# Second cross attention of a two-layer decoder: products in three float32r parts, transposes in row halves, outputs one step later

## Chip, cores and metric

The kernel runs on 1 core of one Trainium2 chip. The metric is the device time in microseconds (us), median of several runs. The whole program, two decoder layers, is one launch; the change is in one of its six stages.

## The reference

x is 2 x 1024 x 256 in float32, ctx is 2 x 154 x 256. Each of six blocks is added to x: a gated delta-rule attention (A), a cross attention (B), experts (C); then a local attention (D), a second cross attention (E) and a mixture of 32 experts (F). The change is in E:

```
def _L1_xattn_ref(Q, K, V, attn_mask, Wq, bq, Wk, bk, Wv, bv, Wo, bo):   # H = 256, NH = 16 heads, DK = 16
    q, k, v = proj(Q, Wq, bq), proj(K, Wk, bk), proj(V, Wv, bv)           # to (b, NH, S, DK)
    scores = jnp.einsum('bhqd,bhkd->bhqk', q, k) / jnp.sqrt(jnp.float32(DK))
    scores = jnp.where(attn_mask[:, None, :, :], jnp.float32(-1000000000.0), scores)
    attn = jax.nn.softmax(scores, axis=-1)
    ctx = jnp.einsum('bhqk,bhkd->bhqd', attn, v)
    return ctx.transpose(0, 2, 1, 3).reshape(b, -1, NH * DK) @ Wo.T + bo
x = x + _L1_xattn_ref(_layernorm(x, axis=-1), ctx_1024, ctx_1024, mask, ...)
```

## The kernel before

The stages run in the order A to F. Every engine walks through the same written list `order` and does its part of each entry, so the order of the list is the order of every engine's queue; engines wait for each other by semaphores. Stage E works on 16 tiles n of 128 rows of x, in 32 steps g: step g holds 8 of the 16 heads of tile g // 2, as two groups j of four heads, and r = 0 to 3 names the four heads of a group, which lie at partitions 32 r. Each head is padded to 32 rows, so the query weights are 256 x 512.

What the entries of `order` do:

- `key`, `value`: products of ctx with the weights, once. `query n4, m`: 128 of the 512 query columns for four tiles, 2 products of 512 columns in float32; ScalarE adds the bias and writes Q. Each float32 product shows in the trace as two matmuls.
- `score g`: for each r a mask product (L2417) into bank r and then the scores of 8 heads (L2425). VectorE takes the maxima of the four banks (L2491); `exp g, r` is ScalarE's exponential, two instructions for each r (L2542), into P. Bank r is free for the next step once its exp is done.
- `turn g, r`: 4 transposes of P (L2436) into one bank; ScalarE copies r = 0, 1 to PT, VectorE r = 2, 3 (L2497). `mix g`: 32 matmuls of values by PT (L2447), copied to OT by ScalarE; `across g`: two transposes back (L2455); VectorE divides by the sums (L2505, L2506) into AO.
- `flip n`: transposes of AO (L2461), copied to AOT by ScalarE (L2562). `out n`: the output product (L2466), added to X by VectorE (L2513).
- `stat`, `norm`, `ln` with the letter F: the layer norm for the next stage, two tiles at a time. `stat`: VectorE's statistics (L262, L265), then six small instructions of GpSimd (L284 to L221) that make rs. `norm`: VectorE's normalisation (L275), which waits for rs. `ln`: TensorE's transposes and ScalarE's copy to XT. The last pair of tiles of stage E's own layer norm is done inside E (`norm`, `ln` with the letter E).
- `bias`: GpSimd adds the output bias to X (L2577).

The scores use banks 0 to 3. Turns, mixes, flips, across, outputs, queries and layer norms use banks 4 to 7 in turn, each as one entry (`i = 4 + turns % 4`), and TensorE waits until the bank's last user has been emptied.

The steps are a software pipeline. In step g TensorE does turn g - 1 (r = 0, 1), mix g - 2, score g, in even steps flip n = g // 2 - 2, turn g - 1 (r = 2, 3), across g - 2, and then in even steps out n, in odd steps up to 23 a query. The four queries of the first tiles come right after the keys. Below, a step starts where its first mask product starts.

Stage B, the first cross attention, and stage F already have products in three float32r parts (L1283, L2676), and stage B has transposes in row halves (L1348), with 16 heads of 64.

## Time and profile before

| | us |
|---|---|
| median of 3 runs | 2528.76 (2523.03 to 2533.08) |
| the profiled execution | 2528.92 |
| its span | 2527.1 |
| stage E, first key product to last X add | 1694.94 to 1910.67 |
| TensorE busy over the whole span | 2246.4 (89%) |
| VectorE, ScalarE, GpSimd busy | 1596.7, 1165.5, 737.1 |
| mean granted clock of TensorE | 0.94 |

Times in the rows below are in us from the span's start. In a timeline row the columns are start, duration until the last of the instructions ends, engine, line, operation and tiles, count, and in brackets the engine's idle time before them and what ended it. PE is TensorE, PEld its weight loads, DVE VectorE, ACT ScalarE, POOL GpSimd.

### The profile page before, as it was taken

The page shows a single profiled execution, that of the slowest core. Times are in us where ns is not written, and L with a number is a line of the kernel's source. Part 1 is how long each engine was busy: PE and PEld are TensorE (multiplying, and loading weights), DVE is VectorE, ACT ScalarE, POOL GpSimd, SP SyncE. Part 2 cuts the span into 40 slices and gives each one's busy share as a digit, 9 for nine tenths or more (in the row PEclk, how much of TensorE's full clock was granted, in tenths as well). Part 3 has the DMA queues.
Part 4 walks back from the last instruction along what each step waited for, and adds up shares of the span by engine and source line. Part 5 has one row for each costly group of instructions (what it writes and reads, how often), then busy time and mean ns, then how long its engine had stood idle before and what let it go on. Part 6 is the DMA issues. An engine that isn't in the chain of part 4 may idle for free. (4 is left out here: it accounts for less than half of the span.)

```text
span 2527.1 us, 63640 instructions
## 1 busy us (share of the span) xinstructions
PE 2246.4 (89%) x26627; PEld 1868.0 (74%) x26627; DVE 1596.7 (63%) x3513; ACT 1165.5 (46%) x3240; POOL 737.1 (29%) x866
## 2 busy tenths in 40 slices
PE   5798989999898999946997689989997899999998
PEld 4677877777785888835886466667776788888887
DVE  6666676667653566546773455655666777777776
ACT  4435444443423777612553366656664233333332
POOL 2334243333423444331664523420101001110110
PEclk9799999999999999967999799999998899999999
DMA  5001010100101100021442300000000000000001
GB/s 162 1 11 36 27 36 11 36 27 11 66 3 60 62 19 19 19 76 39 123 108 47 88 2 2 2 2 2 2 2 20 13 26 26 26 21 24 26 7 34
DMA packets 87966, 83.44 MB, mean 33 GB/s; under 512 B 27264, under 2 KB 83456, under 8 KB 86272
## 3 DMA queue, kind: packets, MB, share of 16 engines
q1 hardware_dynamic: 81536, 70.98, 8.9%
q0 software_dynamic: 6144, 8.39, 2.0%
q8 instruction: 210, 3.44, 0.6%
q14 instruction: 76, 0.62, 0.1%
HBM read 68.71 MB, written 10.65 MB: 31 GB/s over the span
## 5 line engine op out<-in xcount | busy, mean ns | idle before, releaser
L2676 PE MATMUL bank<-f_XH,f_wp 128*128 128x512 f32 x1088 | 364.6, 396 | 5.9 <-DVE f_XL L2786 5.9
L797 DVE SCALAR_TENSOR_TENSOR a_acc<-a_praw,a_convw,a_acc 128x256 f32<-128x256 f32 x345 | 206.2, 599 | 99.2 <-ACT a_acc L957 91.0
L2676 PEld LDWEIGHTS bank<-f_XH,f_wp 128*128 128x128 f32 x1088 | 208.4, 192 | 48.5 <-issue 5.0
L2676 PEld LDWEIGHTS bank<-f_wp,f_Hp 128*128 128x128 f32 x1632 | 214.3, 191 | 27.5 <-DVE X L2813 16.0
L2676 PE MATMUL bank<-f_wp,f_Hp 128*128 128x256 f32 x1632 | 218.5, 283 | 16.2 <-DVE X L2813 15.4
L2676 PE MATMUL bank<-f_XL,f_wp 128*128 128x512 f32 x544 | 215.9, 397 | 0.0
L2860 POOL TENSOR_TENSOR f_wp<-wa,f_wp 128x768 fp32r<-128x768 f32 x34 | 62.9, 1850 | 521.5 <-ACT f_wp L2826 521.5
L2811 DVE SCALAR_TENSOR_TENSOR X<-bank,f_w,X 128x256 f32<-128x256 f32 x512 | 211.4, 476 | 0.0
L2849 ACT ACTIVATE f_Hp<-f_H 128x512 fp32r<-128x512 f32 x136 | 85.9, 632 | 223.8 <-DVE f_H L2798 223.8
L2847 ACT ACTIVATE f_G<-bank 128x512 f32<-128x512 f32 x136 | 81.3, 598 | 165.4 <-PE bank L2676 165.4
L594 PE MATMUL bank<-XT,wa 128*128 128x256 f32 x512 | 155.2, 434 | 0.3 <-ACT a_acc L957 0.3
L2800 DVE TENSOR_TENSOR f_Hp<-f_H,f_Hp 128x512 fp32r<-128x512 f32 x136 | 94.2, 692 | 94.9 <-ACT f_Hp L2849 94.9
L684 PE MATMUL bank<-wa 64*64 64x64 f32 x2560 | 108.1, 229 | 48.8 <-DVE wa L894 35.2
L2798 DVE TENSOR_TENSOR f_H<-bank,f_G 128x512 f32<-128x512 f32 x136 | 94.0, 691 | 80.0 <-PE bank L2676 80.0
L684 PEld LDWEIGHTS bank<-wa 64*64 64x64 f32 x2560 | 89.3, 139 | 72.6 <-DVE wa L894 45.5
L2156 DVE TENSOR_REDUCE d_mx<-bank 128x2 f32<-128x512 f32 (+1 forms) x128 | 75.2, 650 | 105.2 <-PE bank L2091 105.2
L1024 ACT ACTIVATE wa<-bank 128x256 f32<-128x256 f32 x160 | 58.4, 386 | 155.9 <-PE bank L684 155.1
L2226 ACT ACTIVATE d_P<-bank,d_mx 128x256 f32<-128x256 f32 (+1 forms) x256 | 95.0, 479 | 75.1 <-DVE d_mx L2156 75.1
L2676 PEld LDWEIGHTS bank<-f_XL,f_wp 128*128 128x128 f32 x544 | 104.7, 192 | 16.8
L894 DVE COPY_PREDICATED wa<-masks,bank 128x512 f32<-128x512 uint8 x128 | 91.4, 729 | 37.8 <-PE bank L698 37.5
L698 PE MATMUL bank<-wa 64*64 64x64 f32 x2560 | 112.2, 232 | 2.1 <-ACT wa L1024 2.1
L1509 POOL TENSOR_TENSOR b_P<-b_P,b_rec 128x616 f32<-128x616 f32 x64 | 77.7, 1213 | 116.6 <-DVE b_rec L1418 116.6
(390 smaller groups left out, 5520.2 us busy)
## 6 DMA issues: line engine op xcount, KB each, us to landing
wa<-in_c_w SPq DMA_DIRECT2D x64, 256.0 KB, 3.4
wa<-in_f_gu SPq DMA_DIRECT2D x34, 256.0 KB, 2.7
wb<-grown SPq DMA_DIRECT2D x4, 1536.0 KB, 7.0
a_KQg<-grown SPq DMA_DIRECT2D x4, 1536.0 KB, 6.5
wa<-in_f_d SPq DMA_DIRECT2D x34, 128.0 KB, 2.8
a_E<-decays SPq DMA_DIRECT2D x16, 256.0 KB, 4.0
X<-in_x SPq DMA_DIRECT2D x4, 512.0 KB, 5.2
wa<-in_a_wqkv SPq DMA_DIRECT2D x1, 2048.0 KB, 8.8
```

Source lines behind the costliest of these rows:

```text
L594: i = t.e.matmul(b.ap[:, 0:B * BT_].rearrange("p (b t) -> p b t", b=B), wqkv[:, j, c * P:(c + 1) * P], xt, start=j == 0, stop=j == KD - 1, ...
L684: i = t.e.matmul(heads(b.ap)[both(bb), h, :], nt[c % 2][both(bb), h, :], xx[c % 2][both(bb), 0, h, :], start=True, stop=True, tile_positio ...
L698: i = t.e.matmul(heads(b.ap[:, H * R:])[both(bb), h, :], y[both(bb), h, :], xt[both(bb), h, :], start=True, stop=True, tile_position=(bb * ...
L797: i = v.e.scalar_tensor_tensor(A_, praw[:, c, :, j:j + BT_], convw[:, c, j:j + 1], A_, ALU.mult, ALU.add)
L894: i = v.e.copy_predicated(xx[c % 2], masks[:, l].unsqueeze(2).broadcast_to([P, 2, H, R]), b.ap.rearrange("p (w h r) -> p w h r", w=2, h=H))
L2226: i = c.e.activation(Pm[of(g, r)][:, j, lo:], pair(b.ap)[:, j, lo:], ACT.Exp, bias=mx[:, of(g, r), j:j + 1])
L2676: i = t.e.matmul(out_, lhsT[x], rhs[y], start=n == 0 and k == 0, stop=n == 2 and k == nk - 1, skip_group_check=True)
L2798: v.e.tensor_tensor(hid[i][:, :], up.ap, gate[i][:, :], ALU.mult).then_inc(up.emptied, 1)
L2800: v.e.tensor_tensor(hp[i][:, 1], hid[i][:, :], whole(hp[i][:, 0]), ALU.subtract).then_inc(parts_ready.sem, 1)
L2811: i = v.e.scalar_tensor_tensor(X[:, n, :], part, w_[:, n, e_:e_ + 1], X[:, n, :], ALU.mult, ALU.add)
L2847: c.e.activation(gate[i][:, :], b.ap, ACT.Silu).then_inc(b.emptied, 1)
L2849: c.e.activation(hp[i][:, 0], hid[i][:, :], ACT.Copy).then_inc(high_ready.sem, 1)
```

## The change

Queries and outputs: each float32 operand is split into a high part (a copy in float32r by ScalarE) and a low part (the rest, by a subtraction), and a product is the sum of three float32r products, low x high, high x low and high x high. `weights` entries split wq and wo and `inputs` entries split four tiles of XT, each with a ScalarE copy and a GpSimd subtraction; AOT is split by ScalarE's copy and a VectorE subtraction from the bank.

Turns: an entry `turn g, h` covers r = 2h and 2h + 1, and each transpose is done as two of 64 rows in the upper and the lower half of the array, into two banks, one for each half. ScalarE copies the bank of the first half, VectorE that of the second, for every turn.

Order: out n moves from the end of the even step to the odd step after it, behind the scores (where the flip is in even steps). The stat entries of the next stage move with it, from even to odd steps; norm and ln stay where they are. ScalarE's exponentials r = 1 to 3 come behind the second turn. The first four queries move behind the values, GpSimd's memsets behind the first two splits, and there is one more step at the end.

```
+            wqh, wql = (t_(n, [P, KD, MT * P], F32R) for n in ("wqh", "wql"))
+            woh, wol = (t_(n, [P, KD, D], F32R) for n in ("woh", "wol"))
+            XH_, XL_ = ([t_(f"X{n}{i}", [P, KD, 4 * P], F32R) for i in range(2)] for n in "HL")
+            AOTh, AOTl = ([t_(f"AOT{n}{i}", [P, KD, P], F32R) for i in range(2)] for n in "hl")
...
-            PT = [t_(f"PT{i}", [HALF, 2, 2, P]) for i in range(NPB)]
+            PT = [t_(f"PT{i}", [HALF, 2, 2, 2, P]) for i in range(NPB // 2)]
...
-            order = [("key", m) for m in range(MT)] + [("query", 0, m) for m in range(MT)]
+            order = [("weights", 0), ("inputs", 0)] + [("key", m) for m in range(MT)]
             order += [("norm", "E", NT // 2 - 1), ("value", 0, 0), ("value", 0, 1), ("ln", "E", NT // 2 - 1)]
-            order += [("value", 1, 0), ("value", 1, 1)]
-            for g in range(G + 3):
+            order += [("value", 1, 0), ("value", 1, 1)] + [("query", 0, m) for m in range(MT)] + [("weights", 1)]
+            for g in range(G + 4):
                 m, n = g // 2, g // 2 - 2
-                turn = [("turn", g - 1, r) for r in range(4)] if 0 <= g - 1 < G else []
+                turn = [("turn", g - 1, h) for h in range(2)] if 0 <= g - 1 < G else []
                 scores, exps = ([(what, g, r) for r in range(4)] if g < G else [] for what in ("score", "exp"))
-                order += turn[0:2] + [("mix", g - 2)] * (0 <= g - 2 < G)
-                order += scores + exps[0:1] + [("flip", n)] * (g % 2 == 0 and 0 <= n < NT) + turn[2:3] + exps[1:2] + turn[3:4]
-                order += exps[2:4] + [("across", g - 2)] * (0 <= g - 2 < G)
-                if g % 2 == 0:
-                    order += [("out", n)] * (0 <= n < NT) + [("stat", "F", n // 2)] * (0 <= n < NT - 1 and n % 2)
-                elif g // 8 + 1 < NT // 4:
-                    order += [("query", g // 8 + 1, g % 8 // 2)]
-                if g % 4 == 3 and g > 4:
+                order += turn[0:1] + [("mix", g - 2)] * (0 <= g - 2 < G)
+                order += scores + exps[0:1] + [("flip" if g % 2 == 0 else "out", n)] * (0 <= n < NT) + turn[1:2] + exps[1:4]
+                order += [("across", g - 2)] * (0 <= g - 2 < G)
+                if g % 2:
+                    order += [("stat", "F", n // 2)] * (0 <= n < NT - 1 and n % 2)
+                    order += [("query", g // 8 + 1, g % 8 // 2)] * (g // 8 + 1 < NT // 4)
+                if g % 8 == 0 and g // 8 + 1 < NT // 4:
+                    order += [("inputs", g // 8 + 1)]
+                if g % 4 == 3 and 0 <= (g - 7) // 4 < NT // 2 - 1:
                     order += [("norm", "F", (g - 7) // 4)]
                 if g % 4 == 0 and 0 <= g // 4 - 2 < NT // 2 - 1:
                     order += [("ln", "F", g // 4 - 2)]
...
+                elif what == "turn":
+                    for half in range(2):
+                        at[s + (half,)] = banks[4 + turns % 4]
+                        at[s + (half,)].turn(*k, half)
+                        turns += 1
+                    continue
...
+            def three(t, out_, lhsT, rhs, first, last):
+
+                for n, (x, y) in enumerate(((1, 0), (0, 1), (0, 0))):
+                    i = t.e.matmul(out_, lhsT[x], rhs[y], start=first and n == 0, stop=last and n == 2, skip_group_check=True)
+                return i
...
+                        continue
+                    if what == "turn":
+
+
+                        _, g, h = s
+                        for half in range(2):
+                            free(t, *s, half)
+                        for r in range(2):
+                            emptied(t, "score", g, 2 * h + r)
+                            for j in range(2):
+                                for hf in range(2):
+                                    for half, rows_ in enumerate(halves):
+                                        b = at[s + (half,)]
+                                        i = t.e.transpose(by_group(b.ap)[:, r, j, hf, :],
+                                                          Pm[of(g, 2 * h + r)][rows_, j, hf * HALF:(hf + 1) * HALF],
+                                                          ident[rows_, rows_], tile_position=(rows_.start, 0))
+                                        if (r, j, hf) == (1, 1, 1):
+                                            i.then_inc(b.filled, 1)
...
                     elif what == "query":
                         _, n4, m = s
-                        ln_emptied(t, "E", 2 * n4)
-                        ln_emptied(t, "E", 2 * n4 + 1)
+                        t.wait_ge(w_low.sem, w_low.at[0,])
+                        t.wait_ge(x_low.sem, x_low.at[n4,])
+                        cols = slice(m * P, (m + 1) * P)
                         for j in range(KD):
-                            i = t.e.matmul(b.ap, wq[:, j, m * P:(m + 1) * P], XT[:, j, n4 * 4 * P:(n4 + 1) * 4 * P],
-                                           start=j == 0, stop=j == KD - 1, skip_group_check=True)
+                            i = three(t, b.ap, (wqh[:, j, cols], wql[:, j, cols]), (XH_[n4 % 2][:, j, :], XL_[n4 % 2][:, j, :]),
+                                      j == 0, j == KD - 1)
...
-                        for r in range(4):
-                            emptied(t, "turn", g, r)
+                        for h in range(2):
+                            for half in range(2):
+                                emptied(t, "turn", g, h, half)
...
                     elif what == "out":
                         n = s[1]
                         emptied(t, "flip", n)
+                        t.wait_ge(w_low.sem, w_low.at[1,])
                         for j in range(KD):
-                            i = t.e.matmul(b.ap[:, 0:D], AOT[n % 2][:, j, :], wo[:, j, :], start=j == 0, stop=j == KD - 1,
-                                           skip_group_check=True)
+                            i = three(t, b.ap[:, 0:D], (AOTh[n % 2][:, j, :], AOTl[n % 2][:, j, :]), (woh[:, j, :], wol[:, j, :]),
+                                      j == 0, j == KD - 1)
...
+                    elif what == "turn":
+                        _, g, h = s
+                        b = at[s + (1,)]
                         if g > 1:
                             filled(v, "mix", g - 2)
-                        filled(v, *s)
-                        v.e.tensor_copy(PT[of(g, r)][:], square(b.ap)).then_inc(b.emptied, 1)
+                        filled(v, *s, 1)
+                        v.e.tensor_copy(PT[of(g, 2 * h) // 2][:, :, :, :, halves[1]], by_group(b.ap)).then_inc(b.emptied, 1)
...
+                    elif what == "flip":
+                        n = s[1]
+                        v.wait_ge(out_high.sem, out_high.at[n,])
+                        v.e.tensor_tensor(AOTl[n % 2][:, :, :], b.ap[:, 0:D].rearrange("p (k c) -> p k c", k=KD),
+                                          whole(AOTh[n % 2][:, :, :]), ALU.subtract).then_inc(b.emptied, 1)
...
+                    if what == "weights":
+                        raw, high, low = weights[s[1]]
+                        c.e.activation(high[:, :, :], raw, ACT.Copy).then_inc(w_high.sem, 1)
+                    elif what == "inputs":
+                        n4 = s[1]
+                        ln_emptied(c, "E", 2 * n4)
+                        ln_emptied(c, "E", 2 * n4 + 1)
+                        if n4 > 1:
+                            filled(c, "query", n4 - 2, MT - 1)
+                        c.e.activation(XH_[n4 % 2][:, :, :], XT[:, :, n4 * 4 * P:(n4 + 1) * 4 * P], ACT.Copy).then_inc(x_high.sem, 1)
+                    elif what == "key":
...
+                    elif what == "turn":
+                        _, g, h = s
+                        b = at[s + (0,)]
                         if g > 1:
                             filled(c, "mix", g - 2)
-                        filled(c, *s)
-                        c.e.activation(PT[of(g, r)][:], square(b.ap), ACT.Copy).then_inc(b.emptied, 1)
+                        filled(c, *s, 0)
+                        c.e.activation(PT[of(g, 2 * h) // 2][:, :, :, :, halves[0]], by_group(b.ap), ACT.Copy).then_inc(b.emptied, 1)
...
+                        c.e.activation(AOTh[n % 2][:, :, :], b.ap[:, 0:D].rearrange("p (k c) -> p k c", k=KD),
+                                       ACT.Copy).then_inc(out_high.sem, 1)
...
-                g.e.memset(V[:, :, :, :, AD + 1:], 0.0)
-                g.e.memset(V[:, :, :, :, AD:AD + 1], 1.0).then_inc(cleared, 1)
                 g.wait_ge(w_in, 144)
                 for s in order:
-                    if s[0] == "stat":
+                    if s[0] == "weights":
+                        raw, high, low = weights[s[1]]
+                        g.wait_ge(w_high.sem, w_high.at[s[1],])
+                        g.e.tensor_tensor(low[:, :, :], raw, whole(high[:, :, :]), ALU.subtract).then_inc(w_low.sem, 1)
+                    elif s[0] == "inputs":
+                        n4 = s[1]
+                        g.wait_ge(x_high.sem, x_high.at[n4,])
+                        g.e.tensor_tensor(XL_[n4 % 2][:, :, :], XT[:, :, n4 * 4 * P:(n4 + 1) * 4 * P], whole(XH_[n4 % 2][:, :, :]),
+                                          ALU.subtract).then_inc(x_low.sem, 1)
+                    elif s == ("key", 0):
+                        g.e.memset(V[:, :, :, :, AD + 1:], 0.0)
+                        g.e.memset(V[:, :, :, :, AD:AD + 1], 1.0).then_inc(cleared, 1)
+                    elif s[0] == "stat":
                         ln_pool(g, s)
...
```

## Rows read from the trace of the kernel before

**Rows 1.** Windows of steps 0 to 3, 4 to 30, and the end. Columns: window, length, then busy time (instructions) of PE, PEld, DVE, ACT, POOL, granted clock, DMA share, GB/s.

```profile
1710.06:1731.65 21.59, 19.78 (x245) 13.93 (x244) 11.34 (x27) 15.23 (x44) 0.00 (x0) 1.00 0.01 2
1731.65:1897.08 165.43, 161.87 (x2042) 121.53 (x2039) 104.32 (x268) 114.50 (x327) 17.59 (x42) 1.00 0.01 2
1897.08:1910.67 13.59, 10.72 (x134) 7.97 (x130) 7.35 (x21) 5.75 (x16) 1.71 (x6) 1.00 0.01 1
```

**Rows 2.** Windows of step 6 and of step 7.

```profile
1743.90:1749.94 6.04, 5.88 (x81) 4.61 (x77) 4.32 (x11) 4.06 (x12) 0.00 (x0) 1.00 0.01 3
1749.94:1756.15 6.21, 6.21 (x78) 4.37 (x75) 4.30 (x13) 4.38 (x12) 2.93 (x7) 1.00 0.00 0
```

**Rows 3.** Timeline of step 6.

```profile
1745.27 0.44 PE L2461 MATMUL bank<-wide,e_AO 128*128 128x128 f32 x2
...
1745.45 1.64 DVE L2491 TENSOR_REDUCE e_mx<-bank 128x2 f32<-128x308 f32 x4 [2.98 <-PE bank L2425]
1745.54 1.04 PE L2436 MATMUL bank<-wide,e_P 128*77 128x128 f32 x8
1745.96 0.67 ACT L2542 ACTIVATE e_P<-bank,e_mx 128x154 f32<-128x154 f32 x2 [1.54 <-DVE e_mx L2491]
...
1746.52 0.38 ACT L2562 ACTIVATE e_AOT<-bank 128x256 f32<-128x256 f32 x1
1746.78 1.80 ACT L2542 ACTIVATE e_P<-bank,e_mx 128x154 f32<-128x154 f32 x6
...
1747.00 1.27 DVE L2497 COPY e_PT<-bank 77x512 f32<-77x512 f32 x2
1747.92 1.07 PE L2436 MATMUL bank<-wide,e_P 128*77 128x128 f32 x8
...
1748.42 0.29 DVE L2506 TENSOR_TENSOR e_AO<-bank,e_rec 128x128 f32<-128x128 f32 x1
...
1748.92 1.08 PE L2447 MATMUL bank<-e_PT,e_V 77*32 77x128 f32 x32
```

**Rows 4.** Timeline of stage B: a turn in row halves, the next mix, the copy.

```profile
1060.29 0.71 PE L1348 MATMUL bank<-wide,b_P 64*77 64x64 f32 x16
...
1060.93 1.09 PE L1364 MATMUL bank<-b_PT,b_V 77*64 77x128 f32 x16
1061.07 0.59 ACT L1486 ACTIVATE b_PT<-bank 77x512 f32<-77x512 f32 x1 [2.45 <-PE bank L1348]
```

**Rows 5.** Timelines: float32r products of stage F, a query in float32.

```profile
2104.21 0.62 PE L2676 MATMUL bank<-f_XH,f_wp 128*128 128x512 f32 x2
...
2105.11 1.59 PE L2676 MATMUL bank<-f_wp,f_Hp 128*128 128x256 f32 x12
...
1752.45 1.88 PE L2408 MATMUL bank<-XT,wb_d 128*128 128x512 f32 x4
```

**Rows 6.** Timeline of steps 6 and 7: statistics, the last of rs, norm.

```profile
1749.28 0.75 DVE L262 BATCH_NORM_STATS2 stats<-X 128x6 f32<-128x256 f32 x2
...
1752.32 0.20 POOL L221 TENSOR_TENSOR rs<-rs 128x2 f32<-128x2 f32 x1
...
1754.76 0.73 DVE L275 TENSOR_SCALAR xn<-X,mv,rs 128x256 f32<-128x256 f32 x2
```

**Rows 7.** Timelines of the stage's start and last X add; one group of the page.

```profile
1699.23 3.48 DVE L275 TENSOR_SCALAR xn<-X,mv,rs 128x256 f32<-128x256 f32 x1 [2.19 <-POOL rs L221]
...
1700.07 2.49 POOL L2577 TENSOR_TENSOR X<-X,e_bo 128x512 f32<-128x512 f32 x2
...
1910.25 0.42 DVE L2513 TENSOR_TENSOR X<-X,bank 128x256 f32<-128x256 f32 x1 [2.33 <-PE bank L2466]
...
L2860 POOL TENSOR_TENSOR f_wp<-wa,f_wp 128x768 fp32r<-128x768 f32 x34 | 62.9, 1850 | 521.5 <-ACT f_wp L2826 521.5
```

**Rows 8.** Timelines of stage F's start and of stage B, each behind idle time.

```profile
1914.72 0.77 PE L2676 MATMUL bank<-f_XH,f_wp 128*128 128x512 f32 x1 [4.58 <-DVE f_XL L2786]
...
1064.76 0.52 PE L1348 MATMUL bank<-wide,b_P 64*77 64x64 f32 x4 [2.01 <-POOL b_P L1509]
```

More of the change, by code:

```diff
@@ L2348, in stage_e @@
                     continue
+                if what == "weights":
+                    w_high.mark(s[1])
+                    w_low.mark(s[1])
+                    continue
+                if what == "inputs":
+                    x_high.mark(s[1])
+                    x_low.mark(s[1])
+                    continue
+                if what == "flip":
+                    out_high.mark(s[1])
                 if what == "bias":
@@ L2370, in stage_e @@
             pair = lambda ap: ap[:, 0:2 * S2].rearrange("p (h n) -> p h n", h=2)
[L2371 removed]
+            halves = [slice(0, P // 2), slice(P // 2, P)]
+            by_group = lambda ap: ap[0:HALF, :].rearrange("p (r a b c) -> p r a b c", r=2, a=2, b=2)
             def sync(y):
@@ L2385, in tensor @@
                     what, b = s[0], at.get(s)
-                    if what in ("exp", "bias", "stat", "norm"):
+                    if what in ("weights", "inputs", "exp", "bias", "stat", "norm"):
                         continue
@@ L2430, in tensor @@
                         continue
-                    elif what == "turn":
-                        _, g, r = s
-                        emptied(t, "score", g, r)
-                        for j in range(2):
-                            for hf in range(2):
-                                i = t.e.transpose(square(b.ap)[:, j, hf, :],
-                                                  Pm[of(g, r)][:, j, hf * HALF:(hf + 1) * HALF], ident)
                     elif what == "mix":
@@ L2538, in scalar @@
                         if g > 1:
-                            filled(c, "turn", g - 2, r)
+                            for half in range(2):
+                                filled(c, "turn", g - 2, r // 2, half)
                         c.wait_ge(max_ready.sem, max_ready.at[g, r])
```

19 lines of the change are left out of this document (8 added, 11 removed).

## The prediction

> **What bounds the kernel now.** First the windows of the second cross attention (stage E), cut where the score work of steps 0, 4 and 31 starts: between 1731.65 and 1897.08 us TensorE is busy for 161.87 of 165.43 us at a full clock, ScalarE for 114.50, VectorE for 104.32 [rows 1]. Windows of one step each give step 6 (even) 6.04 us, with 5.88 of TensorE, and step 7 (odd, with a query) 6.21, all of it TensorE [rows 2]. So TensorE sets the pace, and cheaper TensorE work pays until something else ends last. What that would be is read from the timeline of step 6 [rows 3], as offsets from its start S = 1743.90. VectorE sits idle for 2.98 us until the scores are there; its four maxima run from +1.55 to +3.10. ScalarE starts the exponentials at +2.06, two for each quarter r, 0.28 apart (0.67 less the 0.39 of one alone); the AOT copy goes in at +2.62 and ends at +3.00.
>
> **Prices.** Sixteen half transposes, the content of one new turn, take 1060.93 - 1060.29 = 0.64 us in stage B, and the copy of their bank starts 0.78 after them [rows 4]; the eight whole ones take (1.04 - 0.27)/7 x 8 = 0.87 [rows 3]. A float32r product of 256 columns takes (1.59 - 0.28)/11 = 0.12, one of 512 columns 0.62 - 0.39 = 0.23 [rows 5]. So an output costs 6 x 0.12 = 0.70 and a query 6 x 0.23 = 1.37, where the four float32 parts of a query now take (1.88 - 0.59)/3 x 4 = 1.72 [rows 5]. Were TensorE to stay the bound, the gain would be 64 turns x 0.23 = 14.7, 16 queries x 0.35 = 5.6, and 16 outputs x 0.6 = 9.6 (now about 1.3 from the end of the across before it, near 1746.62, to the next turn at 1747.92, its wait for AOT in it): 30 us. That is rival 1.
>
> **The steady steps.** Pieces that stay: scores 1.37 (S to the flip at 1745.27), flip 0.27, mix 1.02 (1748.92 to the next S) [rows 3], across 0.21. A VectorE copy of a turn's bank ends after 0.68, the next instruction starts after 0.60; a ScalarE copy 0.59 [rows 4] and, an estimate, 0.49.
> *Even step:* scores, flip, second turn and across leave TensorE idle from +2.50. ScalarE now has a turn copy between the first and the second quarter of exponentials: AOTh takes its place to +2.88, the copy to +3.37, and the second quarter is done at +3.37 + 0.28 + 0.39 = +4.04. VectorE has AOTl, new, at the 0.42 of the X add [rows 7], from +3.10 to +3.52, then its half of the turn, +3.50 to +4.18. TensorE's first turn of the next step needs the flip's bank (four banks go round, and it is the fourth user after the flip), free at +3.57; it turns the first quarter, waits for the second until +4.09, ends at +4.41, and the mix ends the step at 5.43. Gain 0.61 on 6.04.
> *Odd step with a query:* output and query now share a step. TensorE has done the across at +2.97 (1.37 + 0.70 + 0.64 + 0.21 and a gap of 0.05), but the query takes the bank of the output, and VectorE empties that only behind its four maxima: 1.52 + 1.55 + 0.42, so +3.54. Then 1.37, turn 0.64, mix 1.02: 6.57. Loss 0.36 on 6.21. Without a query (the steps from 25) the second quarter of exponentials ends last again: 5.43.
> *Even step with a layer norm* (4 transposes, 0.41): its bank is the fourth after the flip's, so it starts at +3.57; turn and mix follow when VectorE has emptied the turn's bank (+4.18) and AO (+4.62): 5.89.
> Steps 4 to 30 are 8 plain even ones, 6 with a layer norm, 10 odd with a query, 3 without: 43.4 + 35.3 + 65.7 + 16.3 = 160.8 against the 165.4 of [rows 1]: 4.7 won.
>
> **The statistics.** An output comes a step later and takes its statistics along, from step 4k+2 to 4k+3, where the norm of the same tiles already stands. VectorE's norm waits for GpSimd's rs, which is ready 1752.52 - 1749.28 = 3.24 us after the statistics start [rows 6]. Today VectorE does step 7's first turn and maxima in that time; now nothing of its work lies between. Statistics at +4.63, rs at +7.87, then the two norms, 0.73 [rows 6]: VectorE is free at +8.65. Queued behind it are its half of the next step's first turn and that step's maxima, for which ScalarE's exponentials wait, and TensorE's second turn needs the bank of the first. After a step with a query (6.57) the maxima are due at 6.57 + 1.52 = 8.09 and start at 9.25, 1.15 late, five times; after step 27 (5.43) 2.29 late. Sum 8.0. Steps 4 to 30 come to -4.7 + 8.0 = +3.4.
>
> **The start.** Today four queries (7 us of TensorE) stand between keys and values and cover VectorE's norm of the last tiles. Its first instruction took 3.48 us, where two take 0.73 [rows 6]: it ended at 1702.71, when GpSimd's run of memsets and two additions of 1.27 was over (1702.56) [rows 7]. In the new order TensorE does the keys, two value groups (to about 1700.9) and stands before that norm. GpSimd, free at about 1699.2 as now, has two subtractions of 1024 elements, each 2.43 by the slope from 512 elements (1.27) to 768 (1.85) [rows 7], and memsets of 1.1, without a gap to 1705.2. If VectorE gets in only behind them, as today, the norm ends at 1705.7; then layer norm 0.45, values 1.75, four queries 5.5, last Q copy 0.9: step 0 starts near 1714.35 instead of 1710.06 [rows 1], +4.3. TensorE will have been idle for 4.8 us; after 4.58 us of idle its first 512-column product took 0.77 [rows 8] against 0.39 [rows 5], so 1.7 more for some 3.4 us of work at half pace. Start: +6.0. The lower bound is a norm that ends at 1703.04 as now: +1.7.
> The Trainium skill ("GPSIMD Engine Reference", Specifications) says that GpSimd shares its SBUF interfaces with VectorE and contends with instructions in a two-port mode or with two SBUF inputs. The 3.48 us agree. The page doesn't say who goes first between two GpSimd instructions that follow each other at once, on which +1.7 or +4.3 hangs.
> Steps 0 to 3: step 1's query waits for the low part of the next four tiles (ScalarE about 1.04 behind the exponentials, GpSimd 2.43), +0.8; steps 2 and 3 have no output and save 1.0. Together -0.2.
>
> **The end.** From step 31's scores to the end of the last X add are 13.59 us [rows 1]. New: the norm of step 31 holds VectorE to +8.65, its half-turn copy ends at +9.33, the last turn runs from 9.4 to 10.0, its copy to 10.84, the mix to 11.9, output 14 to 12.6, the last AO to 13.8, then flip, AOTh to 14.7, AOTl to 15.1, output 15, X add to +16.6: +3.0. TensorE idles for 3.7 us in it, so again 1.7 for the clock: +4.7.
>
> **Sum.** 6.0 - 0.2 + 3.4 + 4.7 = 13.9 us. The profiled execution took 2528.92 us (its span 2527.1), 0.16 above the median of the runs, 2528.76: I forecast 2528.8 + 13.9, so 2543. Stage F isn't touched and starts, as now, from the last X add.
>
> **Rivals.**
> 1. *TensorE stays the bound*: bank and copy waits hide, and 30 us come off, less start and end (10.7): 2510. For it: 161.87 of 165.43. Against: the chain above. It decides if the query's bank is free before +2.97 and the norm doesn't hold up the maxima.
> 2. *The clock falls inside the loop.* In stage B an idle time of 2.01 us came before half transposes at 0.52 for four [rows 8], where sixteen take 0.71 [rows 4]. The steps behind a late norm have idle times of 1.2 and 1.4 us, behind step 27 of 2.3. A step at half pace adds 1.37 + 0.64 + 0.64 + 1.02 = 3.7 us of TensorE time, of which some 3 show; in six steps 18: 2561. Against: most of these idle times are below 2 us.
> 3. *The ends hide*: VectorE gets in early at the start, and the clock holds at both ends: 13.9 - 4.3 - 3.4 = +6, 2535.
> The Trainium skill ("TensorEngine Tiling (Array Packing)", PSUM Bottleneck) warns that tiling speeds up TensorE but not the emptying of PSUM. By it alone the turns' 14.7 us would be worth nothing wherever a copy ends last; the sum above goes by the rows.
>
> **Chances.** Forecast 0.55, rival 1 0.14, rival 2 0.16, rival 3 0.15. A measurement of this kernel can tell 0.5%, 12.6 us (2516.1 to 2541.4). Faster takes most of rival 1: 0.12. Same takes rival 3 and the lower part of the forecast (0.2 us of error a step over 28 steps is 6 us): 0.43. Slower, the upper part and rival 2: 0.45. The range reaches halfway to rival 1, 2522, and to rival 2, 2560. The likeliest case alone: 2534 to 2551.
>
> **What would show it.** Plain even steps of 5.4 us and odd ones with a query of 6.6; the query waiting 0.5 for the X add; VectorE waiting seven times some 2.2 us for rs; new turns at 0.64; step 0 at 1714 to 1716; the last X add of the stage some 14 us later. It is wrong if even steps stay at 6 us (dearer half turns), if two steps take 11 (rival 1), or if the granted clock falls between steps 4 and 31 (rival 2).

## The result, and the profile after

The changed kernel takes 2576.0 us (median of 4 runs, 2570.0 to 2578.52) against 2527.95 (4 runs, 2523.03 to 2533.08): a ratio of 1.0186, 95% interval [1.0159, 1.0213]. It is slower: the interval lies wholly above 1, though it leaves open whether the loss reaches 2%, and the time is above the range on record (2522 to 2560). The profiled execution took 2578.52 us, its span is 2576.7, the mean granted clock 0.923.

Stage E, cut at the same marks as before (first key product, scores of steps 0, 4 and 31, end of the last X add):

| us | before | predicted change | after | measured change |
|---|---|---|---|---|
| first key product to step 0 | 14.90 | +6.0 | 17.59 | +2.7 |
| steps 0 to 3 | 21.59 | -0.2 | 23.68 | +2.1 |
| steps 4 to 30 | 165.43 | +3.4 | 208.52 | +43.1 |
| step 31 to the last X add | 13.59 | +4.7 | 22.49 | +8.9 |
| stage E | 215.5 | +13.9 | 272.3 | +56.8 |

Stage F behind it took 2.3 us more, and the stages ahead of it, whose code is the same, 9.5 less: the first key product is at 1685.7 us instead of 1695.2. In the ten experiments below it lies between 1682.2 and 1692.0, whatever was changed, so that part is put down to the one execution of before that was profiled. 56.8 + 2.3 - 9.5 = 49.6 is the difference of the spans. Nearly all that has to be explained lies in steps 4 to 30.

The windows of the kernel after: steps 4 to 30 whole, steps 5 and 6, the first 10.2 us at a low clock and the 20.5 us behind them, and a stretch from step 25 to the end of the stage.

```profile
1726.95:1935.47 208.52, 192.88 (x2516) 141.74 (x2513) 112.64 (x279) 117.45 (x330) 22.28 (x44) 0.77 0.01 2
1732.43:1739.27 6.84, 6.70 (x103) 4.97 (x99) 3.65 (x9) 4.62 (x13) 0.00 (x0) 1.00 0.01 2
1739.27:1744.81 5.54, 4.79 (x92) 3.45 (x89) 3.66 (x9) 3.83 (x12) 0.00 (x0) 1.00 0.00 0
1756.10:1766.30 10.20, 10.20 (x98) 7.82 (x99) 4.39 (x12) 5.39 (x15) 3.58 (x2) 0.51 0.00 0
1766.30:1786.80 20.50, 17.38 (x280) 12.51 (x278) 12.66 (x32) 12.81 (x37) 2.93 (x7) 1.00 0.01 2
1879.00:1960.00 81.00, 74.66 (x759) 54.59 (x757) 34.67 (x89) 34.86 (x97) 5.65 (x14) 0.50 0.01 2
```

In the first row the granted clock is what matters: 0.77, where [rows 1] show 1.00. Step 5 (odd, with a query) takes 6.84 and step 6 (even) 5.54, near the 6.57 and 5.43 forecast. Then, at 1756.2, inside step 8, the clock goes to its lower level (0.51 in the window, that is 1.2 of 2.4 GHz) for 10.2 us. The same happens at 1786.9, 1817.7 and 1848.4, each for 10.2 us; at 1879.1 it falls and stays low for 88.7 us, into stage F. The five falls lie in steps 8, 12, 16, 20 and 24, the five steps behind a late norm up to there. At the low level a whole step takes 8.2 to 9.2 us, and TensorE is busy for 10.20 of 10.20 us.

What goes before the first fall is read from the timeline of step 8, which starts at 1751.65:

```profile
1752.41 0.19 POOL L221 TENSOR_TENSOR rs<-rs 128x2 f32<-128x2 f32 x1
1752.64 0.73 DVE L275 TENSOR_SCALAR xn<-X,mv,rs 128x256 f32<-128x256 f32 x2 [2.24 <-POOL rs L221]
...
1753.29 0.68 DVE L2543 COPY e_PT<-bank 77x512 f32<-77x512 f32 x1
1753.89 1.62 DVE L2536 TENSOR_REDUCE e_mx<-bank 128x2 f32<-128x308 f32 x4
1754.12 0.77 PE L2434 MATMUL bank<-wide,e_P 64*77 64x64 f32 x16 [0.66 <-DVE e_PT L2543]
...
1755.99 0.88 PE L296 MATMUL bank<-wide,xn 128*128 128x128 f32 x4 [0.75 <-DVE e_AOTl L2558]
...
1756.81 1.30 PE L2434 MATMUL bank<-wide,e_P 64*77 64x64 f32 x16
...
1758.04 1.93 PE L2491 MATMUL bank<-e_PT,e_V 77*32 77x128 f32 x32
```

VectorE stands for 2.24 us before the norm, as forecast, and does its half of step 7's turn and the maxima only then. The maxima start at +2.24 of the step instead of +1.55. TensorE waits 0.66 and 0.75 us, which would be a small matter; but behind them the sixteen half transposes take 1.30 instead of 0.77 and the mix 1.93 instead of 1.08. The waits of stage E (who waited for whom: us, times, the longest) say the same of the norm:

```profile
DVE xn L275 <- POOL rs L221: 17.9, 8, 2.2
PE bank L2434 <- DVE e_PT L2543: 6.1, 5, 1.6
PE bank L296 <- DVE e_AOTl L2558: 3.7, 5, 0.7
```

Eight waits of 2.2: one at the stage's start and the seven forecast. The two rows of TensorE add up to 9.8 us, where 43 were lost.

Every profile here and below is of one execution. That the clock differs between these kernels is no accident of the one that was profiled: its mean over the whole execution is 0.923 to 0.928 in all four runs of the kernel after, and 0.940 to 0.946 in all nine of e1 below.

### The profile page after: what moved, and what is told of

Same layout as the page of the kernel before. It is cut to its first block and busy times, and to the rows that moved or that the text cites. A ratio compares the mean times of both kernels' runs of the same rounds, so it can differ in the third digit from the quotient of the medians.

```text
span 2576.7 us, 64851 instructions
## 1 busy us (share of the span) xinstructions
PE 2277.6 (88%) x27203; PEld 1888.7 (73%) x27203; DVE 1607.6 (62%) x3529; ACT 1171.8 (45%) x3246; POOL 750.5 (29%) x872
## 5 line engine op out<-in xcount | busy, mean ns | idle before, releaser
L684 PE MATMUL bank<-wa 64*64 64x64 f32 x2560 | 108.3, 230 | 48.8 <-DVE wa L894 34.9
L284 POOL TENSOR_SCALAR rs<-mv 128x2 f32<-128x2 f32 x42 | 10.6, 251 | 345.1 <-DVE mv L265 344.5
```

What stands on the lines that cost most here:

```text
L684: i = t.e.matmul(heads(b.ap)[both(bb), h, :], nt[c % 2][both(bb), h, :], xx[c % 2][both(bb), 0, h, :], start=True, stop=True, tile_positio ...
```

## The experiments

Theory A: the norm that stands before its rs makes TensorE idle, the clock falls, and most of the loss is work at the low clock. Theory B: TensorE's work in the new order is too thin everywhere, and the clock would fall without the late norm. Theory C: the stalls themselves are the loss. Rival D: the three-part products pay, and the turns are bound by their copies. (The expectations of e5, e6, e9 and e10 give the letters A and C to other theories, which they state themselves.) In the table the columns are stage E's parts as above, then the median and the ratio to the kernel before on the same chip.

| kernel | to step 0 | 0 to 3 | 4 to 30 | end | median | ratio |
|---|---|---|---|---|---|---|
| before | 14.90 | 21.59 | 165.43 | 13.59 | 2527.95 | 1 |
| after | 17.59 | 23.68 | 208.52 | 22.49 | 2576.0 | 1.0186 |
| e1 norm later | 20.09 | 23.51 | 165.08 | 14.28 | 2529.12 | 1.002 [1.0003, 1.0037] |
| e2 after, filled | 17.54 | 23.12 | 174.80 | 19.96 | 2545.97 | 1.0094 [1.0067, 1.0122] |
| e3 before, late statistics | 15.93 | 21.59 | 182.60 | 17.41 | 2542.73 | 1.0088 [1.0063, 1.0113] |
| e4 out and statistics back | 20.07 | 23.47 | 160.10 | 15.07 | 2524.27 | 1.0004 [0.9992, 1.0016] |
| e5 halves only | 14.90 | 20.72 | 162.69 | 17.48 | 2521.87 | 1.0000 [0.9988, 1.0013] |
| e6 three parts only | 17.57 | 24.06 | 167.90 | 13.84 | 2530.24 | 1.0036 [1.0019, 1.0053] |
| e7 e4 with another start | 15.34 | 22.64 | 163.67 | 17.29 | 2525.59 | 1.0027 [1.0014, 1.0039] |
| e8 e1, query first | 20.21 | 24.42 | 166.40 | 14.26 | 2529.37 | 1.0037 [1.0023, 1.0050] |
| e9 e5, filled late | 14.90 | 20.71 | 159.48 | 16.10 | 2520.69 | 0.9993 [0.9978, 1.0007] |
| e10 e7, filled late | 15.39 | 22.86 | 161.36 | 16.14 | 2524.72 | 1.0007 [0.9991, 1.0024] |

The kernel before had medians of 2523.02 beside e1 to e4, 2521.41 beside e5 to e8 and 2522.77 beside e9 and e10.

**e1: the norm a step later, and the layer norm's transposes (`ln`) two steps later; the rest as after.**

```
-                if g % 4 == 3 and 0 <= (g - 7) // 4 < NT // 2 - 1:
-                    order += [("norm", "F", (g - 7) // 4)]
                 if g % 4 == 0 and 0 <= g // 4 - 2 < NT // 2 - 1:
+                    order += [("norm", "F", g // 4 - 2)]
+                if g % 4 == 2 and 0 <= g // 4 - 2 < NT // 2 - 1:
                     order += [("ln", "F", g // 4 - 2)]
```

> The changed kernel with the norm of the next stage's tiles one step later (end of step 4k+4 instead of 4k+3) and the layer norm's transposes two steps later (4k+6), so that VectorE no longer stands waiting for rs with the next step's copy and maxima behind it. Theory A (the late norm opens idle time on TensorE, the granted clock falls behind each one and stays low, and most of the loss is work at half clock): no fall between steps 4 and 31, which take about 165 us instead of 208.5; time about 2576 - 43 = 2533. Theory B (the clock falls because TensorE's work has become too thin everywhere, whatever the norm does): the falls stay, time 2560 or more. Theory C (the loss is the stalls themselves, not the clock): only the 8 to 10 us of waiting for rs come back, time 2566.

The windows of e1: steps 4 to 30, then steps 8, 9 and 10:

```profile
1729.07:1894.15 165.08, 152.00 (x2517) 111.92 (x2513) 108.48 (x279) 115.88 (x330) 22.40 (x44) 1.00 0.01 2
1753.77:1759.31 5.54, 4.79 (x92) 3.45 (x89) 3.96 (x11) 3.84 (x12) 0.71 (x4) 1.00 0.02 4
1759.31:1766.14 6.83, 6.69 (x103) 4.96 (x99) 4.00 (x10) 5.44 (x14) 3.61 (x2) 1.00 0.01 2
1766.14:1772.05 5.91, 5.14 (x97) 3.78 (x93) 3.66 (x9) 4.20 (x13) 0.00 (x0) 1.00 0.01 3
```

Moving seven norms, with the `ln` entries that follow them, takes 43.4 us off steps 4 to 30, and the clock holds at 1.00 throughout. TensorE has idle times in these steps too:

```profile
1769.78 0.63 PE L296 MATMUL bank<-wide,xn 128*128 128x128 f32 x4 [0.77 <-DVE e_AOTl L2558]
```

Here 0.77 us in step 10 (and 0.74 in step 8, before the turn that ends it) brought no fall, so the length of the single idle time doesn't tell where the clock falls. TensorE is busy for only 152.0 of 165.1 us here, so work that is thin all over does not by itself bring the clock down: against theory B in this form. Without the late norm there is no fall in the loop; e2, which keeps the `ln` entries in their place, tells how the norm acts.

**e2: the norm stays late, and TensorE gets more to do.** In steps 8, 12, 16, ... the flip is multiplied six times and the across five times over into the same banks; the outputs are the same.

```
-                        for j in range(2):
-                            i = t.e.transpose(b.ap[:, j * P:(j + 1) * P], OT[g % 2][:, j, :], ident)
+                        for _ in range(5 if g % 4 == 2 and g > 2 else 1):
+                            for j in range(2):
+                                i = t.e.transpose(b.ap[:, j * P:(j + 1) * P], OT[g % 2][:, j, :], ident)
...
-                        for j in range(KD):
-                            i = t.e.transpose(b.ap[:, j * P:(j + 1) * P], flat[:, j * P:(j + 1) * P], ident)
+                        for _ in range(6 if n % 2 == 0 and n > 0 else 1):
+                            for j in range(KD):
+                                i = t.e.transpose(b.ap[:, j * P:(j + 1) * P], flat[:, j * P:(j + 1) * P], ident)
```

> The changed kernel with the late norm kept, and TensorE given useless work in the steps behind one: in steps 8, 12, ... 32 the two transposes of the flip are issued six times and the two of the across five times, into the same places, which adds some 1.9 us of TensorE work a step in time that it would idle. Theory A: the clock stays up in the loop, the waits for rs stay; steps 4 to 31 take 165 + 8 to 10 = 175 us, time about 2541, although work was only added. Theory C: no faster than the changed kernel, 2576 or more. Theory B: a small part of the falls goes, 2555 to 2576.

The windows of e2: steps 4 to 30 and step 8.

```profile
1732.40:1907.20 174.80, 163.21 (x2625) 123.84 (x2621) 111.91 (x279) 115.97 (x330) 22.32 (x44) 1.00 0.01 2
1757.11:1764.02 6.91, 6.91 (x115) 5.76 (x111) 4.99 (x12) 4.48 (x13) 0.72 (x5) 1.00 0.02 4
```

With 109 more multiplications than after, and the norm as late as there, the loop is 33.7 us shorter, and the clock stays at 1.00. This splits the 43.1: 33.7 are the clock, 9.7 (174.8 - 165.1) the late norm's stalls with the added work's own time in them, and -0.3 the rest. A count in the trace of after gives nearly the same: the clock is low for 4 x 10.2 us and from 1879.1 to the start of step 31 at 1935.47, 97.3 us in all. Steps 25 to 30, all at the low clock, take 53.1 us there and 36.7 in e2, so 97.3 x (1 - 36.7/53.1) = 30. Theory C holds for less than a fourth, theory A for the rest.

**e3: the kernel before with the statistics a step later**, where the norm of the same tiles already stands; turns, products and outputs as before.

```
-                    order += [("out", n)] * (0 <= n < NT) + [("stat", "F", n // 2)] * (0 <= n < NT - 1 and n % 2)
-                elif g // 8 + 1 < NT // 4:
-                    order += [("query", g // 8 + 1, g % 8 // 2)]
+                    order += [("out", n)] * (0 <= n < NT)
+                else:
+                    order += [("stat", "F", n // 2)] * (0 <= n < NT - 1 and n % 2)
+                    order += [("query", g // 8 + 1, g % 8 // 2)] * (g // 8 + 1 < NT // 4)
```

> The kernel before with one edit: the statistics of the next stage's tiles moved from step 4k+2 to 4k+3, ahead of the norm there, as in the change; all products, turns and outputs as before. Theory A as far as the wait goes: 0.9 us late in five steps and some 2 in two, so +8 us without a fall of the clock, 2537; with falls behind each norm +30 or more. Theory B: the norm matters little while TensorE has its full work, within 8 us of the kernel before and no fall.

The timeline of e3's step 8, whose start is 1744.53, and its window:

```profile
1746.42 1.66 DVE L275 TENSOR_SCALAR xn<-X,mv,rs 128x256 f32<-128x256 f32 x2 [2.25 <-POOL rs L221]
...
1748.00 1.62 DVE L2492 TENSOR_REDUCE e_mx<-bank 128x2 f32<-128x308 f32 x4
...
1749.49 2.08 PE L2467 MATMUL bank<-wb_d,e_AOT 128*128 128x256 f32 x4 [2.07 <-ACT e_AOT L2563]
```

```profile
1744.53:1754.51 9.98, 7.91 (x85) 6.37 (x81) 5.22 (x11) 4.68 (x13) 2.71 (x6) 0.83 0.01 2
```

The same late norm in the old kernel costs 17.2 us in the loop, and the median is 0.9% above before's. The row of the 2.07 us shows what had been overlooked: while VectorE waits for rs, the maxima come late (here at +3.47), the exponentials wait for them, and ScalarE's copy of AOT, and so the output, stands behind. Only three short falls (3.4 us each, from 1749.4, 1858.6 and 1886.0) came here. Steps 12, 16 and 20 have none and take 1.9 us more than before; steps 8 and 24 have one and take 3.5 more. So some 12 of the 17.2 are stalls, where 8 had been expected. The clock falls much more in the new kernel, whose steps give TensorE less to do (152.0 us in e1's loop, 161.87 before): that much of theory B holds. The long falls need both, the late norm and the thinner steps.

**e4: output and statistics back in the even step**, the rest as after.

```
-                order += scores + exps[0:1] + [("flip" if g % 2 == 0 else "out", n)] * (0 <= n < NT) + turn[1:2] + exps[1:4]
+                order += scores + exps[0:1] + [("flip", n)] * (g % 2 == 0 and 0 <= n < NT) + turn[1:2] + exps[1:4]
...
-                if g % 2:
-                    order += [("stat", "F", n // 2)] * (0 <= n < NT - 1 and n % 2)
+                if g % 2 == 0:
+                    order += [("out", n)] * (0 <= n < NT) + [("stat", "F", n // 2)] * (0 <= n < NT - 1 and n % 2)
+                else:
```

> The changed kernel with only the move undone: output and statistics again at the end of the even step, behind the across. Three-part products, row halves, splits and the order at the start stay. Theory A: no wait for rs, no falls; an even step takes 5.9 us (output 0.7 behind the AOTl at +3.57), an odd one with a query 5.5, so steps 4 to 31 some 157 us; start and end cost 3 to 6: time 2522 to 2530. Theory B: the falls stay, above 2555.

The windows of e4: steps 4 to 30, one odd and one even step.

```profile
1729.42:1889.52 160.10, 148.17 (x2523) 111.76 (x2519) 109.72 (x284) 113.82 (x330) 22.45 (x44) 1.00 0.01 2
1735.57:1741.13 5.56, 5.56 (x97) 4.20 (x93) 3.32 (x8) 3.85 (x12) 0.00 (x0) 1.00 0.02 4
1741.13:1747.29 6.16, 5.48 (x99) 4.12 (x95) 4.37 (x14) 4.34 (x13) 0.00 (x0) 1.00 0.01 3
```

160.1 against e1's 165.1: the delayed output, with its statistics still in time in both, costs 5.0 us in the loop; 157 had been expected. The odd step with its query is 5.56 with no bank to wait for, the even one 6.16; together 11.72 against 12.38 in e1 and 12.25 before [rows 2].

**e5: the row-half turns alone**, on the kernel before, with the order of the exponentials that belongs to them; the code of the turns is the change's.

```
-                turn = [("turn", g - 1, r) for r in range(4)] if 0 <= g - 1 < G else []
+                turn = [("turn", g - 1, h) for h in range(2)] if 0 <= g - 1 < G else []
...
-                order += turn[0:2] + [("mix", g - 2)] * (0 <= g - 2 < G)
+                order += turn[0:1] + [("mix", g - 2)] * (0 <= g - 2 < G)
...
```

**e6: the three-part products alone**: e4 with the whole turns of the kernel before and their order of exponentials.

```
-                turn = [("turn", g - 1, h) for h in range(2)] if 0 <= g - 1 < G else []
+                turn = [("turn", g - 1, r) for r in range(4)] if 0 <= g - 1 < G else []
...
```

> The kernel before with the row-half turns alone: 16 half transposes into two banks, one copied by ScalarE and one by VectorE, the exponentials r = 1 to 3 behind the second turn. Products in float32, outputs, statistics and the start as before. Theory A (the chain maxima, exponential, turn copy, exponential sets a step once TensorE's work is cheaper, so that cheaper products beyond the turns buy nothing): plain even steps 5.5, odd ones 5.5, layer-norm steps 6.1, steps 4 to 31 some 152 us instead of 165.4, no fall of the clock, time 13 below the kernel before, and below the changed kernel with output and statistics moved back (4 to 31 there 160.1). Rival D (the products are what pays, the turns are bound by their copies): 4 to 31 at 160 or more.

> Three-part products alone: the changed kernel with output and statistics moved back and the whole turns of the kernel before. From durations: odd steps with a query 1.37 + 0.87 + 0.21 + 1.37 + 0.87 + 1.02 = 5.7 instead of 6.21; even ones, where the output now waits for the new subtraction AOTl, 6.2 instead of 6.04. Steps 4 to 31 some 163, the start 5 us longer as in the changed kernel: time 2 to 5 us above the kernel before under Theory A; below it by 3 or more under rival D.

The windows of e5: steps 4 to 30, steps 25 and 26.

```profile
1723.23:1885.92 162.69, 157.67 (x2474) 110.07 (x2471) 105.58 (x270) 112.02 (x328) 17.58 (x42) 0.97 0.01 2
1847.74:1854.16 6.42, 5.27 (x90) 3.79 (x87) 3.32 (x8) 3.67 (x11) 0.00 (x0) 0.86 0.01 1
1854.16:1863.28 9.12, 9.12 (x97) 6.47 (x93) 4.72 (x13) 4.17 (x12) 0.56 (x2) 0.54 0.01 2
```

The windows of e6: an odd step and an even one.

```profile
1734.90:1740.90 6.00, 6.00 (x80) 4.68 (x77) 3.23 (x8) 4.25 (x12) 0.00 (x0) 1.00 0.00 0
1740.90:1747.27 6.37, 5.70 (x82) 4.60 (x79) 4.65 (x12) 4.09 (x12) 0.00 (x0) 1.00 0.01 3
```

It is the halves that shorten the loop: steps of 5.80 and 5.86 in e5, where [rows 2] have 6.04 and 6.21, and a loop of 167.90 in e6, which lacks them, against 160.10 in e4. Rival D asked for a time below before's in e6, and e6 is 8.8 us above it, so D falls; but e5's 162.7 is above the 160 by which the expectation would have spoken for D, and its steps are 0.3 us longer than the 5.5 expected. Neither expectation was met in size (e6: 163 us and 2 to 5 above). The three-part products make the odd step 0.21 shorter and the even one 0.33 longer: the output's products are cheaper, but start only when ScalarE's high part and VectorE's low part of AOT are both there, where one copy had to be waited for. And e5's gain is given back where the queries have run out: there is no late norm in it, and TensorE is busy for 157.67 of the loop's 162.69 us, yet in step 25, where it is busy for 5.27 of 6.42 us, the clock falls, and step 26 takes 9.12 us at 0.54.

**e7: a start that avoids the norm's wait** (on e4: values and first queries ahead of norm and ln, the next inputs ahead of step 0).

```
-            order += [("norm", "E", NT // 2 - 1), ("value", 0, 0), ("value", 0, 1), ("ln", "E", NT // 2 - 1)]
-            order += [("value", 1, 0), ("value", 1, 1)] + [("query", 0, m) for m in range(MT)] + [("weights", 1)]
+            order += [("value", 0, 0), ("value", 0, 1), ("value", 1, 0), ("value", 1, 1)] + [("query", 0, m) for m in range(MT)]
+            order += [("norm", "E", NT // 2 - 1), ("ln", "E", NT // 2 - 1), ("weights", 1), ("inputs", 1)]
...
-                if g % 8 == 0 and g // 8 + 1 < NT // 4:
+                if g % 8 == 0 and 1 < g // 8 + 1 < NT // 4:
```

> The kernel with output and statistics moved back, and another start: all four value groups, then the four queries, then norm and layer norm of the last tiles, and the split of the next four tiles ahead of the steps instead of behind step 0. If the start's loss is TensorE waiting for VectorE's norm behind GpSimd's subtractions, and step 1's query waiting for the low part, step 0 comes 15.5 us after the first key product instead of 20.05, and steps 0 to 3 take 21 instead of 23.5: 7 us less than its parent (2524.3), 2517. If the start is bound by something else, within 3 us of the parent.

The start is 4.7 us shorter than e4's and steps 0 to 3 are 0.8, but there is a fall of the clock at 1860.8, with steps 27 and 28 at 6.42 and 9.05 us and a loop 3.6 us longer than e4's, and two at 1888.2 and 1898.4, with an end 2.2 us longer. The whole is not faster than e4, where 7 us were expected. The loop's code is the same in both from step 1 on, and up to step 26 its steps take the same times; that only e7's profile has the fall shows that such a fall is not fixed by the code around it.

**e8: in e1, the query ahead of the across**, so that it needn't wait for the X add that empties the output's bank.

```
+                order += [("query", g // 8 + 1, g % 8 // 2)] * (g % 2 and g // 8 + 1 < NT // 4)
                 order += [("across", g - 2)] * (0 <= g - 2 < G)
                 if g % 2:
                     order += [("stat", "F", n // 2)] * (0 <= n < NT - 1 and n % 2)
-                    order += [("query", g // 8 + 1, g % 8 // 2)] * (g // 8 + 1 < NT // 4)
```

> The kernel with the norm one step later (steps 4 to 31 at 165.1) and the query issued ahead of the across, so that it takes the bank of the mix and not that of the output. If the odd steps' 6.84 comes from the query waiting for VectorE's X add behind four maxima, they fall to about 6.0 and steps 4 to 31 to 157: time 8 us less than its parent (2529.1), 2521. If the odd steps are bound by their sum of TensorE work or by the exponentials, they stay above 6.6.

The timeline of e8's step 7 (start 1752.47), where the query starts at +2.96:

```profile
1755.43 0.50 PE L2410 MATMUL bank<-e_XH,e_wql 128*128 128x512 f32 x1
...
1757.66 0.70 ACT L2594 ACTIVATE e_Q<-bank,e_bq 128x512 f32<-128x512 f32 x1
...
1758.42 1.08 PE L2491 MATMUL bank<-e_PT,e_V 77*32 77x128 f32 x32 [0.41 <-ACT e_Q L2594]
```

The query gains 0.6 and the mix loses it: it now needs the bank that ScalarE's copy of the query empties, behind its exponentials. Odd steps take 6.96 instead of 6.83; the 6.0 I expected were wrong. The banks are so closely shared that a wait taken from one product went to the next.

**e9 and e10: e5 and e7 with across multiplied eight times over in steps 25, 27, 29, 31 and 32**, where no query is left.

```
+                        for _ in range(8 if g in (23, 25, 27, 29, 30) else 1):
...
```

> The kernel before with the turns in row halves (as in e5_halves_only), and in steps 25, 27, 29, 31 and 32, where the queries have run out, across is multiplied eight times over into the same bank; the outputs are the same. In e5_halves_only steps 4 to 31 took 162.7 us, with steps 25 and 26 at 6.42 and 9.12 us and a fall of the clock at 1852.6. Theory A (what the halves gain is given back by the clock alone, where the queries are gone): no fall between steps 4 and 31, steps 25 and 26 near 5.8, steps 4 to 31 in 158 to 159 us, the tail 13.5 to 14 instead of 17.5, and a time of 2513 to 2515 us, a ratio near 0.997. Rival C (the halves give nothing on the path, the copies set the steps): steps 4 to 31 at 162 to 165 us without a fall, and the time within 2 us of 2522.

> The kernel e7_out_back_start (outputs and statistics back in their step, the norms and the turn of the first inputs behind the first queries), with across multiplied eight times over into the same bank in the same late steps as in e9_halves_fill. e7 took 2525.59 us, with falls of the clock at 1700.7 and 1861.1 and in the tail. Theory A (the late falls took back what the start gained): steps 4 to 31 in about 160 us instead of 163.7, the tail 14 to 15 instead of 17.3, and a time of 2518 to 2521 us; the fall at the start remains. Rival (the falls come with the whole stage's lighter work, whatever the late steps hold): a fall elsewhere between steps 4 and 31, and the time within 2 us of 2525.6.

The windows of e9: steps 4 to 30, steps 25 and 26.

```profile
1727.65:1887.13 159.48, 157.06 (x2517) 111.42 (x2513) 105.73 (x270) 111.56 (x328) 17.59 (x42) 1.00 0.01 2
1852.13:1857.79 5.66, 5.66 (x104) 4.67 (x100) 3.38 (x8) 3.66 (x11) 0.00 (x0) 1.00 0.00 1
1857.79:1863.65 5.86, 5.64 (x96) 4.03 (x93) 4.03 (x13) 3.94 (x13) 0.00 (x0) 1.00 0.01 3
```

More products, and a shorter loop: the late fall is gone, step 26 takes 5.86 instead of 9.12, and steps 4 to 30 are 3.2 us shorter than in e5 (2.3 in e10 against e7). Each of the four is one profile, and e4's loop had no late fall without such work, so that it is the added products that took the fall away is likely here and not shown. The end came to 16.1 in both, not to 14; the clock falls there instead (at 1901.1 and 1900.2). The medians missed what I expected by some 6 and 4 us. e9's stage E is 4.3 us shorter than before's, 0.17%; its ratio, 0.9978 to 1.0007, can't tell that from nothing. No version here is measurably faster than the kernel before.

## Why the prediction was wrong

**The failed step is the weight given to rival 2**, in its two parts: "some 3 show; in six steps 18", and its chance, 0.16, with the ground "most of these idle times are below 2 us". The forecast itself put the clock at nothing between steps 4 and 31. The mechanism was on record, and the price of a step held (steps 25 and 26 take 3.5 and 2.7 us more at the low clock than in e2, for the 3 on record), but there were 97.3 us at the low clock, more than ten steps' worth and not six, and the whole end of 22.49 us after them. The clock did not go back up with the next step: it stayed low for 10.2 us four times and for 88.7 us the fifth. And the ground was no ground: the idle times just before the fall at 1756.2 are 0.66 and 0.75 us, below the 1.2 and 1.4 that I had worked out and far below the 2.01 us of [rows 8]. I had asked how long one idle time was. That doesn't decide it, as e1's 0.77 without a fall shows; what e1 and e2 change is how much TensorE stands in the steps behind a norm, and the falls of the loop go with it. With the measured 33.7 in the loop added to the forecast, and 8.9 instead of 4.7 at the end, rival 2 would have read 2528.8 + 13.9 + 33.7 + 4.2 = 2580.6.

The Trainium skill ("TensorE: Matmul & The Clock Gate", A second HAM failure mode: psum-queue depth-cycling) tells of a kernel that went back and forth between the two clock levels because TensorE idled briefly and often between groups of products. This case's trace agrees, with idle times of 0.66 and 0.75 us ahead of the first of five falls. The prediction should have weighed it.

**The chain in the steady steps** was right in its order. Plain even steps took 5.54 (forecast 5.43), those with a layer norm 5.91 (5.89, e1), odd ones with a query 6.84 (6.57), without 5.69 (5.43, e1). The timeline of step 5, from 1732.43:

```profile
1735.51 0.41 DVE L2564 TENSOR_TENSOR X<-X,bank 128x256 f32<-128x256 f32 x1
...
1735.97 0.50 PE L2410 MATMUL bank<-e_XH,e_wql 128*128 128x512 f32 x1
...
1737.56 0.77 PE L2434 MATMUL bank<-wide,e_P 64*77 64x64 f32 x16
...
1738.26 1.08 PE L2491 MATMUL bank<-e_PT,e_V 77*32 77x128 f32 x32
```

The query starts at +3.54, exactly as worked out, behind the X add. Two terms were too small: the query 1.59 from its first product to the turn (1.37), because its first product takes 0.34 instead of 0.23 to the next and more follows at its end, and the half turn 0.70 (0.64). Over 27 steps e1's loop came to 165.1 where 160.8 were summed; the 4.7 us that I saw won were 0.3.

**The late norm's stalls**: 8.0 forecast, at most 9.7 by e2. VectorE's seven waits of 2.2 us are there.

**The start**: +2.7 for 6.0. The timeline of the kernel after shows GpSimd's two subtractions and the norm:

```profile
1689.71 2.35 POOL L2635 TENSOR_TENSOR e_wql<-wb_d,e_wqh 128x1024 fp32r<-128x1024 f32 x1
1689.80 4.77 DVE L275 TENSOR_SCALAR xn<-X,mv,rs 128x256 f32<-128x256 f32 x2 [2.19 <-POOL rs L221]
...
1692.02 2.39 POOL L2639 TENSOR_TENSOR e_XL<-XT,e_XH 128x1024 fp32r<-128x1024 f32 x1
1694.36 1.05 POOL L2642 MEMSET e_V<- 77x960 f32 x1
...
1694.62 0.66 PE L296 MATMUL bank<-wide,xn 128*128 128x128 f32 x4 [1.77 <-DVE xn L275]
...
1711.07 0.77 PE L2410 MATMUL bank<-e_XH,e_wql 128*128 128x512 f32 x1 [1.10 <-POOL e_XL L2639]
```

Two subtractions of 2.35 and 2.39 (2.43 estimated), and a norm of 4.77 us, where the same two take 0.73 alone: VectorE's last write comes 0.16 behind the second subtraction and not, as forecast, behind the memsets. TensorE idled 1.77 us there and not 4.8, and the clock did not fall at that place. This is not fixed by the code: e2 and e6 have the same start and a norm of 4.76 too, but in e1, e4 and e8, with the same start again, it took 5.60 to 5.75 and ended behind the memsets. In e1:

```profile
1689.55 5.60 DVE L275 TENSOR_SCALAR xn<-X,mv,rs 128x256 f32<-128x256 f32 x2 [2.20 <-POOL rs L221]
...
1695.21 0.66 PE L296 MATMUL bank<-wide,xn 128*128 128x128 f32 x4 [3.70 <-DVE xn L275]
```

There TensorE idled 3.70 us, the clock fell for 3.4 us at 1696.6, and step 0 came 5.2 us later than before: near the +6.0, mechanism included. So the start's term was right for three of six kernels, and why the others escape it stays open. **Steps 0 to 3** cost 2.1 instead of saving 0.2: the wait for the low part is the 1.10 above (0.8 forecast), but from 1708.4 the clock was low for 6.8 us, and step 1 took 9.27 us (6.17 before).

**The end**: +8.9 for 4.7. The prediction put 1.7 us of low clock into it, for 3.4 us of work; the whole end ran at the low clock. In e2, low for some 6 us of its 19.96, it took 2.5 less; e1, at the full clock and without the norm's wait, needs 0.7 more than before. What the wait alone costs there is not separated.

**Rival 1** (TensorE stays the bound) is excluded by the idle time of e1: 152.0 busy of 165.1. **Rival 3** (the ends hide): they did not, but at the start it was half right.

Still open: why the clock went low for 10.2 us four times and then for 88.7, with TensorE busy for 74.66 of 81.00 us in it. No run here varies that alone. Nor did a run keep the norm's wait at the end of the stage with the clock up throughout.

## What to carry to other kernels

When cheaper products take TensorE from the bound, ask first what will then set the pace, and what a fall of its clock would cost. Its mean busy share doesn't tell whether the clock holds: in e1 it was busy for 92% of the loop without a fall, in e5 for 97% with one, and in the kernel after one wait more in every fourth step brought the clock down and doubled the price of the products behind. Price a clock risk by how long the clock may stay down and not by the idle time that starts it, and look at where a stage runs out of filler work (here the queries) before its end. When a producer moves a step, move all that follows from it: statistics that went with the output, before a norm that stayed, made the difference between 165 and 209 us.

## What was not expected of the hardware

- The first fall of the granted clock, to 0.51, had only idle times of 0.66 and 0.75 us in its step ahead of it; e1 has single ones of 0.77, TensorE busy for 92% of its loop, and kept 1.00.
- The clock stayed low for 88.7 us while TensorE was busy for 92% of the time (74.66 of 81.00 us), at half pace.
- Added multiplications made a kernel faster: e2, with 109 more in the loop, took 2545.97 us instead of 2576.0, its loop 174.8 instead of 208.5. (e9's loop, with 43 more, took 159.5 instead of e5's 162.7 in one profile each; the medians don't tell the two apart.)
- A VectorE norm of two instructions took 4.77 us beside two GpSimd subtractions of 1024 elements, against 0.73 alone [rows 6], and ended with the second of them; beside the same work it took 5.60 in e1.
